# When the two halves of a strip's epilogue run: moving layer-norm chains from a late list to an early one in an attention + FFN kernel

## What is computed

```
def _L0_attn_ref(x, Wq, bq, Wk, bk, Wv, bv, Wo, bo):
    q = jnp.einsum('bsd,kd->bsk', x, Wq) + bq
    k = jnp.einsum('bsd,kd->bsk', x, Wk) + bk
    v = jnp.einsum('bsd,vd->bsv', x, Wv) + bv
    scores = jnp.einsum('bqk,bsk->bqs', q, k) / jnp.sqrt(jnp.float32(KD))
    sign_mask = jnp.sign(scores)
    sign_mask = sign_mask + (sign_mask == 0).astype(jnp.float32)
    masked = jnp.where(causal, scores * sign_mask, -jnp.inf)
    weights = jax.nn.softmax(masked, axis=2)
    out = jnp.einsum('bqs,bsv->bqv', weights, v)
    return jnp.einsum('bqv,dv->bqd', out, Wo) + bo

def _L0_ffn_ref(x, kernel, bias, a, b):
    w = simulate_quantize_int4(kernel)
    y = jnp.einsum('bsd,df->bsf', x, w) + bias
    lora = jnp.einsum('bsr,rf->bsf', jnp.einsum('bsd,dr->bsr', x, a), b)
    return y + lora

x = x + _layernorm(_L0_attn_ref(_layernorm(x), ...))
x = x + _layernorm(_L0_ffn_ref(_layernorm(x), ...))
```

## Time and profile before

| what | us |
|---|---|
| median of 2 runs | 4253.45 |
| the two runs | 4118.0 and 4388.91 |
| the profiled execution, its time | 4119.17 |
| its span on the slowest core (core 6) | 4117.6 |
| spans of the 8 cores | 4089.9 to 4117.6 |
| granted TensorE clock, mean of a core | 0.856 to 0.859 |

### The profile page before, as it was taken

The page is one execution under the profiler, slowest core; times in us unless marked ns, Lnnn a source line. Parts: engine busy times, 40 slices in busy tenths (PEclk is TensorE's granted clock), DMA queues, the critical chain, the costliest instruction groups (busy, mean ns, idle before and its releaser), DMA issues.

```text
span 4117.6 us, 56693 instructions; the slowest of 8 cores (4089.9 to 4117.6 us)
## 1 busy us (share of the span) xinstructions
PE 2764.9 (67%) x17129; PEld 1648.6 (40%) x17129; DVE 1353.9 (33%) x2038; ACT 1406.0 (34%) x3137; POOL 407.3 (10%) x725
## 2 busy tenths in 40 slices
PE   2398895555666777777627899655666677777763
PEld 1233342333344455555303333323344445555541
DVE  3435552333432333322322211033333332222223
ACT  0154552223333333333305555222333333333331
POOL 0000000000111111111000000000001111111110
PEclk9999997788889899888758999877888889888986
DMA  4522223112222223333122221312122223233320
GB/s 153 184 90 88 88 67 115 67 52 75 84 76 82 83 88 93 98 95 96 54 86 79 81 73 61 120 41 75 60 64 88 86 92 92 91 96 99 92 64 16
DMA packets 96557, 348.13 MB, mean 85 GB/s; under 512 B 16245, under 2 KB 16373, under 8 KB 94858
## 3 DMA queue, kind: packets, MB, share of 16 engines
q0 software_dynamic: 63680, 220.25, 17.4%
q1 hardware_dynamic: 32586, 124.26, 9.1%
HBM read 266.85 MB, written 77.59 MB: 84 GB/s over the span
## 4 chain that ended last, share of the span: by engine, by line
PE 53%; DVE 20%; ACT 14%; issue 7%; DMA 3%; ACTq 1%; DVEq 1%; POOLq 0%; SPq 0%; POOL 0%
PE SBp L488 10%; PE OTp L874 10%; PE SBp L833 8%; PE EB L716 6%; DVE sqb L194 6%; PE OTp L529 6%; DVE stats L191 5%; PE EB L619 5%; PE EB L677 2%; DVE sqb L215 2%; ACT stats L202 2%; ACT stats L200 2%; ACT t L627 2%; ACT lnT L683 1%; ACT stats L198 1%
## 5 line engine op out<-in xcount | busy, mean ns | idle before, releaser
L874 PE MATMUL OTp<-PT,V_buf 128*128 128x256 bf16 x4352 | 658.5, 302 | 584.0 <-ACT PT L854 584.0
L874 PEld LDWEIGHTS OTp<-PT,V_buf 128*128 128x128 bf16 x4352 | 454.3, 107 | 711.5 <-issue 624.5
L833 PE MATMUL SBp<-Qs,Ktr 128*128 128x256 bf16 x4352 | 633.2, 296 | 47.4 <-DMA Qs<-q_scr 42.9
L488 PE MATMUL SBp<-lnT,wsl 128*128 128x512 bf16 x2048 | 489.4, 404 | 86.4 <-ACT Qs L495 53.2
L895 POOL DMA_DIRECT2D Ktr<-k_scr x544 | 301.8, 555 | 2245.1 <-PE SBp L833 2178.6
L833 PEld LDWEIGHTS SBp<-Qs,Ktr 128*128 128x128 bf16 x4352 | 427.3, 105 | 178.1 <-issue 92.7
L619 PE MATMUL EB<-wsl,OT_sb 128*128 128x512 bf16 x1024 | 286.6, 430 | 128.5 <-ACT t L627 117.7
L488 PEld LDWEIGHTS SBp<-lnT,wsl 128*128 128x128 bf16 x2048 | 208.6, 103 | 361.8 <-issue 151.2
L841 ACT ACTIVATE Sa<-SBp 128x256 f32<-128x256 f32 x544 | 209.0, 384 | 379.7 <-PE SBp L833 356.6
L207 DVE TENSOR_TENSOR stats<-stats 128x1 f32<-128x1 f32 x256 | 40.7, 159 | 904.6 <-ACT stats L205 900.4
L191 DVE TENSOR_REDUCE stats<-t 128x1 f32<-128x1024 f32 x160 | 195.2, 1220 | 417.6 <-ACT t L731 399.2
(11 more groups left out here) (89 smaller groups left out, 2594.9 us busy)
## 6 DMA issues: line engine op xcount, KB each, us to landing
Ktr<-k_scr POOLq DMA_DIRECT2D x544, 256.0 KB, 3.0
xb<-x SPq DMA_DIRECT2D x128, 512.0 KB, 3.5
y<-xb POOLq DMA_DIRECT2D x64, 512.0 KB, 4.0
q_scr<-Qs POOLq DMA_DIRECT2D x32, 512.0 KB, 5.1
k_scr<-Ktr POOLq DMA_DIRECT2D x64, 256.0 KB, 2.9
Qs<-q_scr SPq DMA_DIRECT2D x32, 512.0 KB, 6.0
xb<-fk SPq DMA_DIRECT2D x8, 512.0 KB, 5.6
xb<-wo SPq DMA_DIRECT2D x8, 512.0 KB, 6.2
```

The lines of the kernel that those rows point to most:

```text
L488: E("tensor", lambda e, wreg=wreg, kc=kc, dc=dc, bk_=bk_: e.matmul(out=SBp[:, bk_ * 512:bk_ * 512 + 512], lhsT=wsl[:, wreg * 8192 + dc * 1 ...
L833: E("tensor", lambda e, j=j, dc=dc, sp=sp, qof=qof: e.matmul(out=SBp[:, sp * 512:sp * 512 + 256], lhsT=Ktr[:, (j % 4) * 1024 + dc * 128:(j ...
L874: lst=(last and vc % 2 == 1): e.matmul(out=OTp[b_][:, col:col + 256], lhsT=V_buf[:, j * 1024 + vc * 128:j * 1024 + (vc + 1) * 128], rhs=PT ...
```

## The change

It alters the fractions of the epilogue's pieces and moves chains a1 and b1 from `spill` to `main`, between the chains of half 0. No instruction is added or taken away.

```
-                main.append((0.40, outproj_h(0, 0)))
-                main.append((0.44, outproj_h(0, 1)))
-                main.append((0.48, outproj_h(1, 0)))
-                main.append((0.52, outproj_h(1, 1)))
-                main.append((0.54, lnattn_a(0)))
-                main.append((0.58, lnattn_b(0)))
-                main.append((0.78, ln2t_pe(0)))
-                main.append((0.84, xa_stage(0)))
-                main.append((0.87, ffn_h(0, 0)))
-                main.append((0.90, ffn_h(0, 1)))
-                main.append((0.93, lnffn_chain(0)))
-                spill.append((0.02, lnattn_a(1)))
-                spill.append((0.06, lnattn_b(1)))
+                main.append((0.36, outproj_h(0, 0)))
+                main.append((0.40, outproj_h(0, 1)))
+                main.append((0.44, outproj_h(1, 0)))
+                main.append((0.48, outproj_h(1, 1)))
+                main.append((0.50, lnattn_a(0)))
+                main.append((0.53, lnattn_a(1)))
+                main.append((0.56, lnattn_b(0)))
+                main.append((0.60, lnattn_b(1)))
+                main.append((0.74, ln2t_pe(0)))
+                main.append((0.78, xa_stage(0)))
+                main.append((0.81, ffn_h(0, 0)))
+                main.append((0.85, ffn_h(0, 1)))
+                main.append((0.89, lnffn_chain(0)))
+                spill.append((0.04, ln2t_pe(1)))
+                spill.append((0.07, xa_stage(1)))
                 if st.get("store1_thunk") is not None:
-                    spill.append((0.10, st["store1_thunk"]))
-                spill.append((0.30, ln2t_pe(1)))
-                spill.append((0.34, xa_stage(1)))
-                spill.append((0.34, store_stage(0)))
-                spill.append((0.38, ffn_h(1, 0)))
-                spill.append((0.42, ffn_h(1, 1)))
-                spill.append((0.46, lnffn_chain(1)))
+                    spill.append((0.07, st["store1_thunk"]))
+                spill.append((0.10, ffn_h(1, 0)))
+                spill.append((0.14, ffn_h(1, 1)))
+                spill.append((0.18, lnffn_chain(1)))
+                spill.append((0.28, store_stage(0)))
```

## The result

The changed kernel takes 4139.95 us (median of 12 executions, 4126.32 to 4431.59) against 4118.0 for the kernel before (11 executions). In some executions the cores of a die run at a lower clock and the time is longer (4431.59 us is such a time); ratios are taken from the others alone. The ratio is 1.0049, with a 95% interval of 1.0034 to 1.0064: about 20 us slower, where 48 us faster was forecast. The change stays within 2% and the time lies in the stated range, but the sign is wrong: the change is small, and it is a loss.

The account below looks back on a forecast made before the run. Exponentials queued behind layer-norm chains on in-order ACT keep PE waiting. Per sequence -17.2 us (strips 2 to 15), +12.3 (strip 1) and -19.0 (tail) give -23.9, for two -48: 4071 us against 4119.2, range 3970 to 4145.

Parts of the forecast that it names:

- What bounds the kernel: PV on PE waits 584.0 us for exponentials that stand behind layer-norm chains on in-order ACT.
- The price of a chain, what goes, what comes: Each chain 7.1 us; leaving strip starts saves 12.7 or 8.4 us; entering the middle clump costs 14.2, 12.4 or 9.
- What the new fractions spread: Around f1 and the out-projection: gain 5.5 to 6 us at 20 to 28 iterations, 5 to 2.6 elsewhere.
- The earlier transposes: Half 1's transposes early in the strip: no longer wait at 6 and 8 iterations; no cost counted.
- f0: Near the strip's end, one iteration earlier: saves 2 us at 24 to 32 iterations, loses 4 at 10 to 14.
- Strip 1 and the tail: Per sequence, strip 1 gains two chains, +12.3 us; the tail after the last strip gets shorter, -19.0 us.
- Part 1: Tail's beginning: a1 and b1 of strip 14 now run in strip 15, so an eviction comes about 13.6 us earlier.
- parts 2 and 3: Tail: a1 and b1 ahead of half 0's transpose evictions, +12.7 us; shorter way to half 1's FFN, -18.1.
- Waits that don't decide: Loads of half 1's x tile and K tiles: still covered, so nothing was counted for either.
- Idle only: Rival: leaving the strip's start saves only idle time, 9.6 and 5.2 us; +87 us, 4158 us, chance 0.09.
- Nothing in the strips: Rival: strip gains and losses cancel, only strip 1 and the tail remain; -13 us, 4106 us, chance 0.14.
- The clock rival: Rival: PE's clock stays low behind the four-chain clump, 48 us per slow iteration; over 2% slower from 2.7; chance 0.07.

Follow-up runs that it names:

- the fastest kernel: Changed kernel with its four chains 0.12 apart, f0 at 0.95 up to 20 iterations and 0.88 from 22, f1 at 0.21: 3812 us, ratio 0.9268.
- the move alone: Kernel before with only a1 and b1 moved from the later strip's start into the middle clump, other fractions kept: ratio 1.0134, +55 us.
- the run with two numbers altered: Kernel before with b1 moved from 0.06 to 0.15 and b0 from 0.58 to 0.68: 3887 us, ratio 0.9418.

## Why the prediction was wrong

**What bounds the kernel**: right. PE's wait for exponentials behind chains is the bound; the fastest kernel halves it and takes 300 us less.

**The price of a chain, what goes, what comes**: right in sign and size, but the total hides two misses. The step between chains was 7.0 us as forecast. By itself the move was forecast to cost (+32 us per sequence by its terms; +37 with the fractions of the run that tried it alone), and the move alone measured +35.3 in strips 2 to 15. Within that, strips of 10 and 12 iterations cost 4.7 and 4.5 us where -0.3 was forecast, and those of 18 to 32 together 27.6 where the terms give 32.

**What the new fractions spread**: this is the step that failed: "Gain: 5.5 to 6 us for nt 20 to 28, 5 for 18, 3 for 30 and 32 [...], 2.6 up to 16". These gains sum to about 50 us per sequence (5 x 5.75 + 5 + 2 x 3 + 4 x 2.6). What they measured can be read from the starts of PV: the stretch from f1 to the last out-projection group, less 1.80 us for each iteration in it, 1.72 for each group and 2.36 for each FFN piece (both from undisturbed steps of 3.52 and 4.16 us), summed for one sequence, with median and mean taken as in the table of strip lengths:

| strips by iterations | before | changed | changed, f1 at 0.26 | gain, changed | forecast |
|---|---|---|---|---|---|
| 10 to 16 | 27.7 | 26.6 | 10.5 | 1.1 | 10.4 |
| 18 to 22 | 18.3 | 13.3 | 4.0 | 5.0 | 16.5 |
| 24 to 28 | 13.3 | 5.5 | 1.2 | 7.8 | 17.3 |
| 30, 32 | 8.8 | 4.4 | 0.7 | 4.4 | 6.0 |
| sum | 68.1 | 49.8 | 16.4 | 18.3 | 50.2 |

So the term was 18 and not 50, and these 32 us are as much as the whole error; the other misses, of both signs, nearly cancel. Three things were wrong in it. First, the price of f1 alone, put at 1.7 us from a row of another kind of stall: it is 2.05 (3.85 less 1.80) where one iteration lies between f1 and the last FFN piece, but 3.85 (5.65 less 1.80), mostly with slow matmuls behind, where none does, and the new fractions 0.14 and 0.18 leave none at 10, 16 and 22 iterations. Second, the crowded stretch was priced by the row of 22 iterations (5.8 us), but it costs 4.3 to 4.6 from 24 on. Third, the 2.5 us around a0 weren't there. The idea itself was sound: with f1 alone moved on to 0.26, two iterations and more behind its input from 12 iterations on, the same stretch gains 52 us.

**The earlier transposes**: taken as a gain or as nothing, measured as a new wait of PE at the start of strips up to 24 iterations, 1.3 to 1.9 us in each from 14 on. How much it costs in the strips below 14, where it is longer but much else is in series, stays open.

**f0**: +4 us in each strip of 10 to 14 iterations was forecast, 12 in all; 10.8 was measured. Right. The gain in long strips was right too: 7.0 us at 24 to 28 iterations against 6.

**Strip 1 and the tail**: +12.3 forecast, +13.4 measured; -19.0 forecast, -23.6 measured. Part 1 of the tail was right as far as a difference shows it, parts 2 and 3 were 5 us too small.

**Waits that don't decide**: right. The changed kernel's PE waits for a K tile once, 0.6 us, and never for an x tile.

**The rivals**: none came true as a whole. "Idle only" (4158) came nearest in time, with the right sign for a wrong reason: with the chains gone from the start of the strip with 32 iterations, its PVs follow at 1.79 to 1.85 us (move alone, core 7), so the 8.4 us that the forecast took for it are returned and not only the 5.2 of idle time. "Nothing in the strips" (4106) had the wrong sign. The clock rival needed 2.7 further slow iterations behind a clump and got about one. But the reading that one long clump pays the clock once didn't hold either: it is paid behind every stall inside the clump.

**The forecast's own sum**: its strips of 20 to 28 iterations don't follow from its terms. With +4.0 for the clump, 5.75 of spread and 2 of f0 from 24 on they average -3.0 us, and -1.9 was summed. Added up as stated, the forecast would have been a few us further from what was measured.

The changes, per sequence: +35.3 for the move in strips 2 to 15, -16.0 for the fractions there (the changed kernel less the move alone, where about -50 was forecast), +13.4 for strip 1, -23.6 for the tail: +9.1, for two sequences 18 us, against about 20 measured. The -16.0 is a difference of two kernels and holds the other clumps at 18, 30 and 32 iterations too.

## What to carry to other kernels

Here a short dependent operation on an engine that works in order cost the time between the moment at which the engine reached it and the moment at which its input was ready. So measure that distance before choosing a place: two iterations of unrelated work behind its input made it free here (3.14 us of waiting to none), and two numbers that widened the distance between dependent chains were worth 5.8%, while moving chains to another strip without widening it cost 55 us. When a stall is to be moved, price it as it will be at its new place, with the distance to its input that it has there for every length of the loop: a fraction of the loop that leaves one iteration between two pieces at 20 iterations can leave none at 22.

## What the runs showed of the hardware

After idle times of 3.1 to 14.2 us, 8 matmuls of 256 columns mostly took 1.86 to 1.87 us instead of 1.04 when PE resumed (behind 3.67 to 3.68 us at f1 it was 1.86 in one strip, 1.66 in another and 1.03 in a third), also at each stall inside a clump, although the stalls there are only 3.1 to 3.5 us long; in the move alone the granted clock over the three stalls (4023.9 to 4041.0, core 7) is 0.50, the lower level of 1.2 GHz, and 1.00 right behind (4043.0 to 4047.0). How long it lasts behind the last stall doesn't depend on the number of chains in what the rows show: the second PV took 1.16 us behind a pair, 1.85 behind four chains, and 1.91 behind f1 alone; the third took 1.04 in each.

With the stalls gone the mean granted clock of the cores rose from 0.856 to 0.859 before to 0.879 to 0.882 in the fastest kernel, so a stall costs more than its idle time. In the run with two numbers altered PE's busy time fell from 2764.9 to 2719.5 us with the same instructions. So of the 230 to 240 us that it gained, where 130 to 190 were expected, some 45 are matmuls that ran faster, and the rest is idle time.
